# Half of the token chunks through per-expert tiles of rows, in a fused feed-forward, attention, feed-forward kernel

## The reference

```python
scores = jax.nn.sigmoid(x @ gate_w.T)
sc = scores + gate_bias[None, :]
group_scores = jax.lax.top_k(sc.reshape(T, G, E // G), 2)[0].sum(-1)   # G = 8 groups of 8 experts
_, gidx = jax.lax.top_k(group_scores, TG)                              # 4 groups stay
_, tidx = jax.lax.top_k(masked, K)                                     # K = 8 experts of 64
tw = tw / (tw.sum(-1, keepdims=True) + 1e-20) * SCALE
def body(acc, ws):                                                     # over all 64 experts
    wg, wu, wdn, cw = ws                                               # 128x64, 128x64, 64x128
    hmid = jax.nn.silu(x @ wg) * (x @ wu)
    return (acc + cw[:, None] * (hmid @ wdn), None)
x = x + 0.5 * (y + shared)
```

## Time and profile before

| | us |
|---|---|
| median of 3 runs | 1830.77 |
| the profiled execution | 1831.43 |
| its span, first to last instruction | 1829.7 |
| first feed-forward, from 0 to | 652.8 |
| attention, to | 1206.5 |
| second feed-forward, to | 1829.7 |

### The profile page before, as it was taken

How to read it: one execution, slowest core, us unless ns; L and a number is a source line. 1 busy time by engine, 2 the same in 40 slices (tenths; PEclk the granted TensorE clock), 3 DMA queues, 4 the chain that set the end, 5 groups by cost and what they waited for, 6 DMA issues and landing times.

```text
span 1829.7 us, 30208 instructions
## 1 busy us (share of the span) xinstructions
PE 1781.7 (97%) x9049; PEld 1255.0 (69%) x9049; DVE 1331.9 (73%) x3327; ACT 774.6 (42%) x1971; POOL 36.6 (2%) x84
## 2 busy tenths in 40 slices
PE   5899999999999999999999999879999999999999
PEld 3566666666666667777778777756666666666665
DVE  5777677676776678888888888767677676777765
ACT  3333323233232256767666666633323233232322
POOL 0000000000000000000000000000000000000000
PEclk8999999999999999999999999999999999999999
DMA  9954554455545500000000000034554455544553
GB/s 206 173 122 110 115 117 105 107 115 115 117 100 109 116 1 2 0 0 0 0 0 0 0 0 0 1 82 109 120 118 108 107 122 121 117 104 111 120 124 75
DMA packets 109530, 149.60 MB, mean 82 GB/s; under 512 B 30128, under 2 KB 43056, under 8 KB 109488
## 3 DMA queue, kind: packets, MB, share of 16 engines
q1 hardware_dynamic: 109488, 149.08, 36.9%
HBM read 144.87 MB, written 4.19 MB: 81 GB/s over the span
## 4 chain that ended last, share of the span: by engine, by line
PE 61%; DVE 2%; DMA 0%; issue 0%; ACT 0%; SPq 0%; POOLq 0%; POOL 0%; DVEq 0%
PE banks L521 12%; PE banks L489 7%; PE banks L487 7%; PE banks L488 7%; PE banks L1059 6%; PE banks L1099 5%; PE banks L1080 4%; PE banks L1116 3%; PE banks L1024 2%; PE banks L1063 2%; PE banks L1025 2%; PE banks L1026 2%; PE banks L1043 1%; PE banks L1044 1%; PE banks L1042 1%; DMA f_mix_wide<-mix_rows 0%
## 5 line engine op out<-in xcount | busy, mean ns | idle before, releaser
L592 ACT ACTIVATE f_hid<-banks 128x512 f32<-128x512 f32 x528 | 315.4, 597 | 835.9 <-PE banks L521 831.5
L648 DVE TENSOR_TENSOR f_hid<-banks,f_hid 128x512 f32<-128x512 f32 x528 | 363.9, 690 | 338.0 <-ACT f_hid L592 336.3
L521 PE MATMUL banks<-f_hid,wd 128*128 128x512 f32 x1056 | 540.7, 594 | 10.7 <-DVE f_hid L659 10.6
L487 PE MATMUL banks<-r_xT_hi,wg_hi 128*128 (+1 forms) x528 | 393.0, 744 | 2.4 <-PEq L951 2.4
L659 DVE TENSOR_TENSOR f_hid<-f_mix_wide,f_hid 128x512 f32<-128x512 f32 x512 | 352.9, 690 | 38.4 <-DMA f_mix_wide<-mix_rows 24.3
L521 PEld LDWEIGHTS banks<-f_hid,wd 128*128 128x128 f32 x1056 | 196.8, 188 | 67.6 <-DVE f_hid L659 13.1
L487 PE MATMUL banks<-r_xT_hi,wu_hi 128*128 (+1 forms) x528 | 209.9, 398 | 0.0
L489 PE MATMUL banks<-r_xT_lo,wu_hi 128*128 (+1 forms) x528 | 209.9, 398 | 0.0
L488 PE MATMUL banks<-r_xT_hi,wu_lo 128*128 (+1 forms) x528 | 208.8, 396 | 0.0
L489 PE MATMUL banks<-r_xT_lo,wg_hi 128*128 (+1 forms) x528 | 208.3, 394 | 0.0
L488 PE MATMUL banks<-r_xT_hi,wg_lo 128*128 (+1 forms) x528 | 207.3, 393 | 0.0
(11 more groups left out here) (153 smaller groups left out, 2155.4 us busy)
## 6 DMA issues: line engine op xcount, KB each, us to landing
f_mix_wide<-mix_rows SPq DMA_DIRECT2D x252, 512.0 KB, 6.5
landing<-in_L_ffn_We_gate SPq DMA_DIRECT2D x4, 512.0 KB, 7.1
landing<-in_L_ffn_We_up SPq DMA_DIRECT2D x4, 512.0 KB, 7.8
wd<-in_L_ffn_We_down SPq DMA_DIRECT2D x4, 512.0 KB, 6.8
mix_rows<-r_mixT SPq DMA_DIRECT2D x32, 64.0 KB, 2.1
out<-x_all SPq DMA_DIRECT2D x8, 256.0 KB, 6.7
f_mix_wide<-mix_rows SPq DMA_DIRECT2D x4, 384.0 KB, 5.4
f_mix_wide<-mix_rows SPq DMA_DIRECT2D x4, 128.0 KB, 3.0
```

The costliest lines, as they stand in the source:

```text
L487: nc.tensor.matmul(bank[:, :], hi, rhs_hi, start=start, stop=False)
L521: nc.tensor.matmul(acc[:, :], w["wd"][:, p * P:(p + 1) * P], hid[:, p % HIDS, :], start=(p == 0), stop=(p == PAIRS)).then_inc(down_done, 1)
L592: nc.scalar.activation(hid[:, p % HIDS, :], gate_bank[p % 3][:, :], ACT.Silu).then_inc(silu_done, 1)
L648: nc.vector.tensor_tensor(hid[:, p % HIDS, :], up_bank[p % 3][:, :], hid[:, p % HIDS, :], ALU.mult)\
```

## The change

Of the 8 chunks of each feed-forward, 4 stay *dense* and go through all experts as before. The other 4 are *sparse*: each token's normalised row goes to its 8 experts alone.

- **Dense slots.** The split into high and low parts is gone. Gate, up and down are one float32 matmul each. The weights are kept once, in float32.
- **A plan for the sparse chunks.** Their routing ends with a mask of the chosen experts (23 steps in place of 25). PE counts the tokens of each expert (`count`), DVE rounds the counts up to 128 and sums them (`plan`), and from PE's ranks (`rank`) each token gets 8 row numbers (`place`). `weigh` makes the 8 weights of each token (17 steps for a chunk, one or two in a slot).
- **Scatter.** POOL writes each tile of 128 tokens 8 times into `x_rows` in DRAM, by an indirect DMA of 128 rows of 512 bytes each time: 128 of them for 4 chunks (`dispatch`, half a tile's eight a call). Before, ACT clears `x_rows` with 12 transfers of 1 MB in slots 16 to 49 of the first feed-forward.
- **Quads.** `x_rows` is 48 times 4 tiles of 128 rows; a tile belongs to one expert. With 4 that do the shared expert on the sparse chunks there are 52 *quads*, each with 4 transposes, 4 gate-and-up matmuls (128 rows, 128 columns, the expert's number read from SBUF into a PE register), 2 transposes of the hidden rows, 4 down matmuls (64 by 128), three ACT and three DVE operations, a load of 256 KB and a store of 256 KB to `y_rows`. The loads wait until all 128 scatters have landed. In the first feed-forward the quads stand behind the four dense chunks, in the second behind the first dense chunk.
- **Gather and add.** For each tile of 128 sparse tokens POOL gathers 8 times 128 rows from `y_rows` (128 indirect DMAs for a feed-forward), and DVE adds them to x, weighted, one after the other (128 operations on 128x128). For the first feed-forward this stands in steps 3 to 34 of the attention, for the second in the last three dense chunks.
- **Attention.** q and v are copied by ACT in place of DVE; v's copy comes behind the copies of the turned probabilities. PE's output product stands behind the projection of v. Layer norm, logits and routing for the second feed-forward's sparse chunks and its first dense chunk stand among the steps (4 routing steps in a step of the attention), with an exponential and a reciprocal in place of the sigmoid. From step 49 on POOL dispatches the second feed-forward's rows, 60 of its 128 scatters; the other 68 stand at the start of the second feed-forward.
- **Loads.** Weights are loaded by SP between the spreads of the first chunk, the first 16 experts' gate and up by ACT. The down weights are loaded twice, once for each half of the partitions.

The core of the diff:

```diff
-            def three(bank, kind, p, rhs_hi, rhs_lo, start=True, stop=True):
-                hi, lo = w[kind + "_hi"][:, p * P:(p + 1) * P], w[kind + "_lo"][:, p * P:(p + 1) * P]
-                nc.tensor.matmul(bank[:, :], hi, rhs_hi, start=start, stop=False)
-                nc.tensor.matmul(bank[:, :], lo, rhs_hi, start=False, stop=False)
-                return nc.tensor.matmul(bank[:, :], hi, rhs_lo, start=False, stop=stop)
...
+        def up(g):
+            c, p = divmod(g, SLOTS)
+            x = d.xT[:, c % 2, :]
+            if p == 0 and routes[c].front >= 0:
...
+            nc.tensor.matmul(gate_bank[g % 3][0:rows, :], w["gu"][:, 0, experts, :].rearrange("p e f -> p (e f)"), x,
+                             start=True, stop=True).then_inc(gate_done, 1)
...
+            nc.tensor.matmul(up_bank[g % 3][0:rows, :], w["gu"][:, 1, experts, :].rearrange("p e f -> p (e f)"), x,
+                             start=True, stop=True).then_inc(up_done, 1)
...
+SPARSE = 4
+DENSE = 4
+TILES = (TOPK * SPARSE * CHUNK - E) // P + E
+QUADS_R = -(-TILES // CT)
+ROWS = QUADS_R * CHUNK
+QUADS_ALL = SPARSE + QUADS_R
+PAD = E // 2
+YBUFS, STORE_LAG, GBUFS = 3, 6, 3
+HALVES = (range(0, TOPK // 2), range(TOPK // 2, TOPK))
...
+FIRST = routes_of([(0, True), (1, True), (4, False), (5, False), (6, False), (7, False), (2, True), (3, True)])
+SECOND = routes_of([(0, False), (1, False), (2, False), (3, False), (4, True), (5, True), (6, True), (7, True)],
+                   by_row=SPARSE + 1)
...
+        def dispatch(i):
+            tile, half = divmod(i, 2)
+            k, t = divmod(tile, CT)
+            if t == 0 and half == 0:
+                pool.wait_ge(idx_done, k + 1)
+            for j in HALVES[half]:
+                nc.gpsimd.indirect_dma_start(
+                    x_rows[:, :], bass.IndirectOffsetOnAxis(ap=b.idx[:, f, CT * k + t, j:j + 1], axis=0),
+                    b.xk[:, k, t, :], None).then_inc(scattered, 16)
...
+        def gather(t, js=range(TOPK)):
+            if t >= GBUFS and js[0] == 0:
+                pool.wait_ge(added, added_before + TOPK * (t - GBUFS + 1))
+            for j in js:
+                nc.gpsimd.indirect_dma_start(
+                    g_buf[:, t % GBUFS, j, :], None, y_rows[:, :],
+                    bass.IndirectOffsetOnAxis(ap=b.idx[:, f, t, j:j + 1], axis=0)).then_inc(gathered[t % GBUFS], 16)
...
+        def add(t, js, chunk_of):
+            x = x_all[:, chunk_of[t // CT] * CT + t % CT, :]
+            for j in js:
+                if j == 0:
+                    dve.wait_ge(gathered[t % GBUFS], 16 * TOPK * (times_before[t % GBUFS] + t // GBUFS + 1))
+                    if t % CT == 0:
+                        dve.wait_ge(r.weigh_step, WEIGH_STEPS * (t // CT + 1))
+                else:
+                    dve.wait_ge(added, added_before + TOPK * t + j)
+                nc.vector.scalar_tensor_tensor(x, g_buf[:, t % GBUFS, j, :], b.w8[:, f, t, j:j + 1], x,
+                                               ALU.mult, ALU.add).then_inc(added, 1)
...
+        def load_experts(j):
+            if j < SPARSE:
+                expert[j] = [E] * CT
+                return
+            i = j - SPARSE
+            if i == 0:
+                pe.wait_ge(r.plan_step, PLAN_STEPS - 1)
+            _, expert[j] = nc.values_load_multi_w_load_instructions(
+                b.ids[i:i + 1, :], engines=PE_ONLY, min_val=0, max_val=E,
+                skip_runtime_bounds_check_because="the number of 64 experts that end at or before a tile")
...
+        def gate_up(j):
+            load_experts(j)
+            e = expert[j]
+            pe.wait_ge(xT_copied, j + 1)
+            if j >= 2:
+                pe.wait_ge(hid_done, j - 1)
+            for t in range(CT):
+                wt = w["gu"][:, :, e[t], :] if j < SPARSE else \
+                    w["gu"][:, :, bass.ds(e[t], 1), :].rearrange("p k a f -> p k (a f)")
+                mm = nc.tensor.matmul(B[j % 2][:, t * P:(t + 1) * P], q.xqT[:, j % 2, t * P:(t + 1) * P], wt,
+                                      start=True, stop=True)
+            mm.then_inc(gu_done, 1)
...
+        def turn_hid(j):
+            pe.wait_ge(hid_done, j + 1)
+            if j >= 1:
+                pe.wait_ge(hT_copied[0], j)
+                pe.wait_ge(hT_copied[1], j)
+            for u in range(2):
+                mm = nc.tensor.transpose(C[:, u * P:(u + 1) * P], q.hid[:, j % 2, u * P:(u + 1) * P], w["ident"][:, :])
+            mm.then_inc(hid_turned, 1)
...
+        def down(j):
+            e = expert.pop(j)
+            pe.wait_ge(hT_copied[0], j + 1)
+            pe.wait_ge(hT_copied[1], j + 1)
+            if j >= 2:
+                pe.wait_ge(y_read, j - 1)
+            for t in range(CT):
+                wt = w["wd"][0:F, e[t], :] if j < SPARSE else \
+                    w["wd"][0:F, bass.ds(e[t], 1), :].rearrange("p a h -> p (a h)")
+                mm = nc.tensor.matmul(ends[j % 2][:, t * P:(t + 1) * P], q.hidT[:, j % 2, t, :], wt,
+                                      start=True, stop=True)
+            mm.then_inc(y_done, 1)
...
+        def step(j):
+            if ok(j):
+                turn(j)
+            if ok(j - 1):
+                gate_up(j - 1)
+            if ok(j - 2):
+                turn_hid(j - 2)
+            if ok(j - 3):
+                down(j - 3)
...
+        def load(i):
+            if i == 0:
+                sp.wait_ge(r.scattered, 16 * TOPK * CT * SPARSE)
+            if i >= 3:
+                sp.wait_ge(turned, SPARSE + i - 2)
+            sp.dma_start(q.xq[:, i % 3, :, :], rows(x_rows, i)).then_inc(loaded[i % 3], 16)
+        def store(i):
+            sp.wait_ge(y_read, SPARSE + i + 1)
+            sp.dma_start(rows(y_rows, i), q.yq[:, i % YBUFS, :, :]).then_inc(y_stored[i % YBUFS], 16)
...
+FIRST_AT = {1: 3, 2: 12, 3: 20, 4: 28, 5: 36, 6: 47, 7: 76}
+COUNT_AT, PLAN_AT, PLACE_AT, PLACE_GAP, WEIGH_AT = 50, 51, 56, 5, 62
+SCATTER_AT = [58 + (5 * i) // 2 for i in range(2 * SPARSE * CT)]
+CLEAR_AT = tuple(range(16, 52, 3))
...
+            for c in range(DENSE):
+                for n in range(GROUPS):
+                    spread(c, n)
+                    if (c, n) == (0, 0):
+                        load_gate_up(sp, 2)
+                    elif (c, n) == (0, 1):
+                        load_down(2)
+                        load_tiles(4 * CT, 8 * CT, x_sparse)
+                    elif (c, n) == (0, 2):
+                        load_gate_up(sp, 3)
...
+            def clear_rows(i):
+                flat = x_rows.rearrange("(p n) d -> p (n d)", p=P)
+                n = flat.shape[1] // len(CLEAR_AT)
+                act.dma_start(flat[:, i * n:(i + 1) * n].rearrange("p (a z) -> p a z", z=zero.shape[1]),
+                              zero[:, :].rearrange("p (a z) -> p a z", a=1).to_broadcast([P, n // zero.shape[1],
+                                                                                        zero.shape[1]]))\
+                    .then_inc(zeroed, 16)
...
+            def copy_v(c, k):
+                s, _ = at(c, k)
+                if not (isinstance(c, int) and c == 0 and k < 2):
+                    act.wait_ge(o_done, s - 1)
+                act.wait_ge(proj_done, 3 * s + 3)
+                nc.scalar.copy(v[:, k % 2, :, :], v_bank[:, :].rearrange("p (a n) -> p a n", a=TB))\
+                    .then_inc(v_read, 1)
...
+                    exps(c, k - 1)
+                if k < STEPS or not last:
+                    copy_q(c, k)
+                    copy_k(c, k)
...
+                if soft:
+                    copy_probT(c, k - 1)
+                if k < STEPS or not last:
+                    copy_v(c, k)
...
+                    update_x(c, k)
+                routing(k)
+                t, half = divmod(k - ADD_LAG, 2)
+                if 0 <= t < SPARSE * CT:
+                    add(t, HALVES[half], chunk_of)
+                if live:
+                    maxima(c, k, 1)
...
+            for k in range(STEPS):
+                if k < 2 * SPARSE * CT:
+                    gather(k // 2, HALVES[k % 2])
+                if k >= A_DISPATCH:
+                    dispatch(k - A_DISPATCH)
+                if front_row(k, 6) is not None:
+                    front_rstd(front_row(k, 6))
+                if moments_row(k) is not None:
+                    rstd_of(moments_row(k))
...
+SECOND_AT = {5: 3, 7: 2 * SLOTS + 1}
+Q_AT = 6
+C_FROM, C_GAP = SLOTS + 6, 5
+STORE_AFTER = {(1, 7): 0, (2, 4): 1, (3, 1): 2, (3, 6): 3}
...
+            for i in range(dispatched, 2 * SPARSE * CT):
+                if i == dispatched + 3:
+                    rstd_of(in_dense[0])
+                dispatch(i)
+            rstd_of(among)
+            for side in range(YBUFS):
+                pool.wait_ge(qd.y_stored[side], 16 * len(range(side, QUADS_R, YBUFS)))
+            last = -(-(SECOND_AT[7] - C_FROM) // C_GAP) + 1
+            for t in range(SPARSE * CT):
+                if t == last:
```

(2 more changed lines are left out.)

1812 lines of the change are left out of this document (1147 added, 665 removed).

## The result

The changed kernel takes 2079.5 us (median of 4, 2077.47 to 2084.63) against 1831.3 (4 runs, 1829.75 to 1833.15): the ratio is 1.136, 95% interval 1.134 to 1.138. The forecast was 1731 with 1640 to 1860 around it, so sign and range are wrong. One more instruction of 0.12 us on POOL behind each indirect transfer makes the same change 1716.1 us, ratio 0.938 (0.936 to 0.940), 15 us under the forecast.

What follows compares the result with a forecast made beforehand. PE, busy for 97% of the span, was taken as the bound. First feed-forward 592, attention 591 and second feed-forward 547 sum to 1730 us, plus 1.7 around it, forecast as 1731 against 1831.4, with a range of 1640 to 1860.

Steps and rivals of the forecast that it cites:

- So at 1.4 they cost nothing: POOL's 512 indirect transfers, taken at 1.4 us each, are hidden by other work; every tenth over 1.6 costs.
- the 1.0 us of rows 7: Profiled time of a short POOL operation, read as saying that POOL isn't quick at anything.
- Dense slots: Feed-forwards: three float32 products of 0.85 make a slot 2.55 us; 132 slots, 337 us for each feed-forward.
- Quads: Sparse feed-forward: PE-bound at 3.1 us, including 0.15 per product group and the expert-number load; 52 take 161 us.
- Rival 3: Quads are bound by their chain, not by PE, at 4.5 us each: +146, 1877 us, slower; chance 0.09.
- First feed-forward: 592 us: 29.5 start, 337 dense, 161 sparse, 25 turnings and end, 28 DVE overload, 12 DMA collisions.
- Second feed-forward: 547 us: 337 dense, 161 sparse, 29 as before, 12 for draining and refilling, 8 for DVE.
- Attention: 591 us: 553.7 before, plus 17, 8, 11 and 8, less 7; bounds 545 and 640.
- the 17 us for the full steps: Attention: DVE needs 9.4 us in 17 steps with adds, routing and front rows, 1.0 over the pace each.
- Rival 1: POOL's issue is the bound, at 2.2 us each: 1860 us, slower; decides from about 2.05 us; chance 0.14.
- Rival 4: The cover holds better: DVE and DMA overloads half swallowed, quads at 2.7 us: about 1650 us; chance 0.21.
- Rival 2: Gathers starve in the attention alone, waiting for DVE's scalings of the probabilities: 1776 us; chance 0.10.

Runs made afterwards that it cites:

- a_touch: Changed kernel with a POOL memset of 0.12 us behind each of its 512 indirect transfers: 1716.1 us, ratio 0.938.
- a_fill1: Changed kernel with a short elementwise power of 0.63 us on POOL behind each of its 512 indirect transfers: 1829.6 us.
- a_fill4: Changed kernel with a longer elementwise power of 1.09 us on POOL behind each of its 512 indirect transfers: 1996.2 us, ratio 1.091.
- a_paced: Changed kernel with POOL waiting for the landing of each of its 512 indirect transfers before going on: 2313.5 us.
- b_indirect: Kernel before with 448 indirect POOL transfers of 64 KB that nobody needs, in bursts of 32 in direct succession: 2209.5 us.
- b_touch: Kernel before with 448 unneeded indirect POOL transfers and a POOL memset of 0.12 us behind each: 1834.9 us.
- a_plain: Changed kernel with its 512 indirect transfers replaced by plain POOL ones of 64 KB at fixed rows, so without the routing's sorting: 1709.0 us.

## Why the prediction was wrong

**The step that failed** is POOL's: "So at 1.4 they cost nothing". Its size was nearly right, 1.26 us from one to the next (asked: 1.4, bounds 0.64 and 2.1), and so was what hides it: with the memset no wait of PE for the quads' loads is left. What it left out, put at nothing without a reason, is that an instruction of an engine off the path can hold up what another engine tells the rest: here PE's semaphore raises, 88 of which are recorded over 1 us late. The bounds asked how long POOL is held, not what a transfer does to the others; nothing in the trace of before could show it, since it has no indirect transfer. An operation that no row shows needs a bound for its effect on others too. The price of the omission is 2079.5 - 1716.1 = 363 us. One reading beside it was wrong too: the 1.0 us of rows 7 is that of a power on POOL, and doesn't say that POOL isn't quick at anything, since a memset takes it 0.12.

**The other steps** can be read in a_touch, where the stalls are out (columns as in the earlier trace rows):

```profile
0.00:29.50 29.50, 13.36 (x31) 6.79 (x31) 13.19 (x57) 7.20 (x10) 4.99 (x23) 0.98 0.89 170
29.50:422.40 392.90, 362.70 (x899) 160.53 (x900) 280.37 (x754) 108.82 (x169) 157.31 (x270) 0.97 0.64 160
422.40:567.40 145.00, 144.76 (x1148) 129.89 (x1147) 76.19 (x164) 69.90 (x157) 0.91 (x2) 1.00 0.62 170
567.40:1200.60 633.20, 571.74 (x4617) 439.92 (x4616) 476.62 (x1691) 428.93 (x1462) 230.08 (x426) 0.97 0.08 22
1200.60:1296.70 96.10, 90.37 (x216) 39.69 (x217) 68.77 (x154) 25.33 (x40) 76.97 (x138) 0.96 0.62 154
1296.70:1443.00 146.30, 146.06 (x1160) 131.19 (x1158) 99.02 (x245) 73.36 (x161) 1.59 (x2) 1.00 0.63 173
1443.00:1715.30 272.30, 263.00 (x623) 114.37 (x621) 184.44 (x383) 64.70 (x107) 144.02 (x258) 0.99 0.55 126
```

- **Dense slots**, forecast 2.55. Their products lie like this in a_touch (answers to the earlier trace rows):

```profile
394.87 1.02 PE L789 MATMUL banks<-r_xT_d,gu 128*128 128x512 f32 x2
395.73 1.02 PE L793 MATMUL banks<-r_xT_d,gu 128*128 128x512 f32 x2
396.59 1.02 PE L805 MATMUL banks<-f_hid,wd 128*128 128x512 f32 x2
397.44 1.02 PE L789 MATMUL banks<-r_xT_d,gu 128*128 128x512 f32 x2
```

  397.44 - 394.87 = 2.57: right.
- **Quads**, forecast 3.1 each and 161 us. 145.0 and 146.3: 16 and 15 us less. Each takes 1332.92 - 1330.14 = 2.78 us:

```profile
1330.14 1.06 PE L592 MATMUL banks<-gu,f2q_xqT 128*128 x8
1331.03 0.38 PE L602 MATMUL banks<-ident,f2q_hidq 128*128 128x128 f32 x2
1331.35 1.16 PE L614 MATMUL banks<-wd,f2q_hidT 64*128 x8
1332.43 0.66 PE L567 MATMUL banks<-ident,f2q_xq 128*128 128x128 f32 x4
1332.92 1.06 PE L592 MATMUL banks<-gu,f2q_xqT 128*128 x8
```

  The mis-sized term is what was added for groups of short products and for the load of the experts' numbers: of 0.65 us at most 0.33 is there (2.78 - 2.45). Rival 3 is out: PE is busy for 146.06 of 146.30 us at the full clock.
- **First feed-forward**, forecast 592: 567.4. Of the 25 us, 16 are the quads'. Dense slots and all that waits: 392.9 where 337 + 25 + 28 + 12 = 402 were forecast.
- **Second feed-forward**, forecast 547: 514.7. Of the 32 us, 15 are the quads'; dense 368.4 where 337 + 29 + 12 + 8 = 386 were forecast.
- **Attention**, forecast 591: 633.2, 42 more, inside the bounds of 545 and 640. Four light steps and four with adds and routing, against four of before:

```profile
621.00:655.00 34.00, 33.89 (x285) 26.33 (x283) 29.02 (x100) 26.62 (x91) 18.84 (x36) 1.00 0.12 30
780.00:823.00 43.00, 36.68 (x292) 27.87 (x290) 34.44 (x119) 27.02 (x92) 20.45 (x37) 0.96 0.10 27
```

```profile
899.00:932.40 33.40, 33.40 (x284) 26.25 (x283) 27.64 (x86) 22.77 (x83) 0.89 (x2) 1.00 0.00 0
```

  The light ones take 34.0 / 4 = 8.50 us with q's and v's copies on ACT, 0.09 over the 8.41 of before: some 6 us over 64 steps, where 11 were forecast for v's. The full ones shown take 10.7 on average where 9.4 were forecast, though DVE is busy for 34.4 of 43.0 us. The prediction summed DVE's work and asked whether it fits a step; but DVE's copy of the attention's output stands behind the adds and the routing, and PE waits for it (engine and line, what it waited for: us in total, times, longest):

```profile
PE banks L1174 <- DVE a_oT L1459: 30.7, 18, 3.3
```

  (from 693 to 910 us.) By the starts of v's copies, the six groups of four steps from 694 to 952 us last 41.9 to 44.5 each: 24 steps of 10.7 on average, single ones 8.4 to 14.3, where 17 of 9.4 were counted. So the term that was mis-sized is the 17 us for the full steps. That it is DVE's order that costs is argued from this wait; the one reordering tried made it worse.
- **The sum** of the terms as measured is 567.4 + 633.2 + 514.7 = 1715.3, beside 1730. That a_touch comes so near is luck in part: three errors cancel but for 15 us, -25, +42 and -32.

**The rivals.** Rival 1 (POOL as the bound) did not happen, but a_fill1, a_fill4 and a_paced are its cases at 1.8, 2.3 and 2.95 us, and cost 114, 280 and 597 us beyond a_touch. Rival 4 (quads at 2.7, the overloads half swallowed) is near in the feed-forwards, which are 57 us under the forecast with quads at 2.78, and wrong in the attention. Rival 2 (gathers starved by DVE's scalings) fell: in a_touch a gather takes POOL 0.977 us in the attention and 0.999 in the second feed-forward, and the 44 transfers of 512 that took over 1.1 us all lie in the feed-forwards. By the Trainium skill ("SBUF — State Buffer", the "DVE blocks DMA" trap) VectorE's 2-port operations keep GpSimd from writing descriptors; these rows show no such loss (a scaling lasts 0.28 to 0.35 us in the trace of before, so a wait for one would be no longer). The disturbance here goes another way, from POOL's transfers to PE's raises. By the Trainium skill ("DMA: Bandwidth & Descriptors", the anatomy of one DMA) most of the 2 us of a transfer lie behind its issue; a_paced agrees, 1.96 of 2.95 us for a scatter; the whole is longer than the 2.15 us that the prediction estimated from the page.

## What to carry to other kernels

If several engines idle at once, one of them waiting for another that is long done, and the page names an unknown queue on a single core, look at when semaphores were raised and at what POOL does then. Count only raises that have a record of their own: a missing record looks like a late raise. Don't let POOL issue indirect DMAs in direct succession: put any short instruction of POOL between each two, here 0.12 us that fit into a gap, and measure, since a memset behind each fourth was enough in one kernel and useless in the other. A new kind of operation off the path needs one run by itself inside the old kernel before the whole change is built on it: b_indirect would have shown 0.85 us each at once.

## What the runs showed of the hardware

- While POOL issues indirect DMAs in direct succession (one per 1.26 us), PE's semaphore raises come late and in order, as from a queue: by 56 us in the stall shown, with 5.60 us from one to the next there. Such steps are 12 in the whole trace of the changed kernel, and others (4.9 and 4.2 us, in b_indirect 7.0 and 7.7) stand beside them, so 5.60 is no constant. 8.6 us behind POOL's last transfer (1559.9 to 1568.5) the backlog of nine comes 0.04 us apart. ACT's and DVE's raises aren't shown to be late. Bytes (64 or 8 KB) and rows (128 or 16) don't matter.
- A memset of 0.12 us between each two takes this away, and the median distance of two transfers stays at 1.26 us (b_touch 1.264, b_indirect 1.266).
- POOL is held 0.54 us by a plain DMA of 64 KB and 0.98 by an indirect one, 0.87 with 16 rows; a scatter's landing comes 1.96 us behind POOL's part (a_paced).
- The unrolled code, with 140 packets of instructions instead of 42, shows no cost: a_plain has PE busy for 93% of 1707 us with it.
